# Expert rows scattered to their tokens' places tile by tile, and the final sums fed by eight plain loads and split over three engines

## The reference, cut to what matters

```python
g = flat @ shared_gate.T
u = flat @ shared_up.T
shared_out = jax.nn.sigmoid(g) * u @ shared_down.T
weights = jax.nn.softmax(flat @ router_w.T, axis=-1)
top_w, top_idx = jax.lax.top_k(weights, 2)
...
he = jax.nn.sigmoid(ge) * ue
de = jnp.einsum('nei,ehi->neh', he, wd)
routed = (comb[:, :, None] * de).sum(axis=1)
return x + shared_out + routed
```

## Time and profile before

| | |
|---|---|
| median of 3 runs | 720.56 us (720.54 to 720.6) |
| the profiled execution's own time | 722.7 us |
| its span, first to last instruction | 720.9 us |
| PE busy | 629.1 us, 87% |
| DVE busy | 516.7 us, 72% |
| ACT busy | 449.4 us, 62% |
| POOL (GpSimd) busy | 321.6 us, 45% |
| mean granted clock of TensorE | 0.941 of 2.4 GHz |
| indirect DMAs issued by POOL | 39 (L1424) and 32 (L1604) |
| first L1424 starts, last L1563 starts, last L1614 starts | 566.59, 663.89, 716.07 us |

### The profile page before, as it was taken

One profiled execution on the slowest core, in us unless ns is written; L12 is line 12 of the kernel. 1 busy time (PEld: TensorE's weight loads), 2 busy tenths in 40 slices (PEclk: granted clock), 3 DMA queues, 4 the chain that ended last, 5 costly groups with the idle time before them and its releaser, 6 DMA issues.

```text
span 720.9 us, 11913 instructions
## 1 busy us (share of the span) xinstructions
PE 629.1 (87%) x3851; PEld 259.9 (36%) x3864; DVE 516.7 (72%) x959; ACT 449.4 (62%) x609; POOL 321.6 (45%) x444
## 2 busy tenths in 40 slices
PE   4888999999999999999999996778899899998960
PEld 3622332332333323323323321133454456665420
DVE  2497888888888888888888898743638444444684
ACT  3553877877877878877877876664432367774000
POOL 5584326346346355355443403331734544430664
PEclk9856999999999999999999997689999999999995
DMA  8543254364364354363334320041895233342454
GB/s 289 175 124 95 71 153 139 83 169 132 86 168 130 93 163 129 93 162 108 108 94 129 108 89 30 31 109 49 201 223 125 51 113 117 118 114 78 147 174 146
DMA packets 65611, 88.61 MB, mean 123 GB/s; under 512 B 12576, under 2 KB 46112, under 8 KB 64528
## 3 DMA queue, kind: packets, MB, share of 16 engines
q1 hardware_dynamic: 60992, 69.64, 32.1%
q0 software_dynamic: 4560, 18.22, 11.0%
HBM read 63.75 MB, written 32.74 MB: 134 GB/s over the span
## 4 chain that ended last, share of the span: by engine, by line
PE 66%; DVE 13%; ACT 8%; issue 6%; DMA 4%; POOL 2%; another core or an unknown queue 0%; SPq 0%; POOLq 0%; ACTq 0%; DVEq 0%
PE PS L859 16%; PE PS L831 10%; PE PS L640 8%; PE PS L766 8%; PE PS L1489 6%; ACT E L845 5%; DVE MX L772 5%; PE PS L719 4%; PE PS L1067 4%; PE PS L1550 3%; PE PS L1317 3%; DVE ST L393 2%; DMA E<-scr_ys,SL 2%; PE PS L1447 1%; ACT BIG L508 1%
## 5 line engine op out<-in xcount | busy, mean ns | idle before, releaser
L772 DVE TENSOR_REDUCE MX<-PS 128x1 f32<-128x512 f32 x512 | 326.7, 683 | 53.9 <-PE PS L766 53.3
L845 ACT ACTIVATE E<-PS 128x1024 f32<-128x1024 f32 x256 | 259.5, 1021 | 80.3 <-PE PS L831 79.5
L859 PE MATMUL PS<-E,BIG 128*32 128x512 f32 x1024 | 140.4, 621 | 3.3 <-ACT E L845 3.2
L766 PE MATMUL PS<-BIG 53*128 53x512 f16 x512 | 123.1, 400 | 17.5 <-DVE MX L772 17.2
L831 PE MATMUL PS<-BIG 55*128 55x512 f16 x512 | 103.1, 398 | 24.2 <-ACT E L845 20.7
L674 POOL TENSOR_TENSOR ML<-BIG,ML 128x512 f32<-128x512 f32 x30 | 38.3, 1277 | 142.6 <-ACT BIG L650 142.6
L831 PEld LDWEIGHTS PS<-BIG 55*128 55x128 f16 x512 | 24.7, 93 | 169.6 <-ACT E L845 99.7
L650 ACT ACTIVATE BIG<-PS,BIG 128x256 f32<-128x256 f32 x64 | 36.1, 565 | 36.1 <-PE PS L640 29.5
L1424 POOL DMA_INDIRECT CT<-scr_yr,IX x39 | 37.0, 949 | 43.9 <-PE PS L1447 36.9
L1511 DVE SCALAR_TENSOR_TENSOR E<-WP,PS 128x352 bf16<-128x352 f32 x39 | 20.3, 521 | 50.4 <-ACT WP L1501 46.7
L1489 PE MATMUL PS<-BIG,CT 128*128 x312 | 54.2, 318 | 0.6 <-issue 0.4
(11 more groups left out here) (211 smaller groups left out, 850.8 us busy)
## 6 DMA issues: line engine op xcount, KB each, us to landing
scr_parts<-WP SPq DMA_DIRECT2D x96, 128.0 KB
BIG<-scr_parts SPq DMA_DIRECT2D x64, 192.0 KB
BIG<-in_we POOLq DMA_DIRECT2D x8, 1088.0 KB, 14.1
scr_u<-ML SPq DMA_DIRECT2D x32, 256.0 KB, 2.1
scr_ys<-XN SPq DMA_DIRECT2D x19, 256.0 KB
X<-in_x SPq DMA_DIRECT2D x8, 512.0 KB, 6.3
CT<-in_ctx SPq DMA_DIRECT2D x8, 512.0 KB, 5.9
ML<-scr_u SPq DMA_DIRECT2D x16, 256.0 KB
```

What stands on the lines that cost most here:

```text
L766: e.matmul(PS[:, yi[name] % 3, :], QK[rows, qb(u), 0, j0 + jj, 128 * tt:128 * tt + 128], QK[rows, qb(u), 1, j0 + jj, :], start=True, stop= ...
L772: e.tensor_reduce(MX[:, g % 2, c:c + 1], PS[:, yi[name] % 3, :], AX.X, ALU.max)\
L845: e.activation(E[:, st, 2 * jj:2 * jj + 2, :], PS[:, slot(name):slot(name) + 2, :], ACT.Exp, scale=1 / 1024).then_inc(s["rc"], 1)
L859: ins = e.matmul(PS[32 * hh:32 * hh + 32, AVB, :], VT[:, b % 2, st, 4 * (g % 4) + hh, :], E[:, st, hh, :], start=(st == 0), stop=(st == 3))
```

## The change

- The list of slots carries a sign: `tok` and `ntok` are the token number plus one, positive for choice 0 and negative for choice 1, and zero for a padding slot. `IX` (which token to gather) is made from it in three DVE steps, and four more (`places`) make `OX`: the row of `scr_ys` where the result belongs. `scr_ys` now has rows 0 to 2047 for choice 0 of each token, 2048 to 4095 for choice 1, and a row of its own for every padding slot.
- SP's plain stores of pairs are gone. POOL stores each tile by an indirect DMA (`place`), due at tb+j+1.48 and tb+j+1.92. An eviction waits for both stores of the pair before last.
- The 32 gathers of the tail are gone. SP loads `scr_ys` in 8 plain loads of 512 KB, once all stores have landed; choice 1's rows of a block of four row tiles come before choice 0's.
- Each row tile's sum is shared by three engines: ACT multiplies choice 1 by its weight (`weigh`), POOL adds that to `X` (`second`), DVE multiplies choice 0 by its weight and adds it (`first`). For row tiles 0 to 7 DVE's addition of the shared result comes first of all; for tiles 8 to 15 (`LATE`) it comes last.

```diff
+LATE = 8
-    ys = nc.dram_tensor("scr_ys", (128 * NTILE, T), BF, kind="Internal").ap()
+    ys = nc.dram_tensor("scr_ys", (2 * 2048 + 128 * NTILE, T), BF, kind="Internal").ap()
...
-        GB = [E[:, i, :, :].rearrange("p a t -> p (a t)").bitcast(BF)[:, 512 * j:512 * j + 512]
-              for i in (0, 3) for j in range(8)]
+        GB = [[big[:, 2048 * (2 * m + c):2048 * (2 * m + c) + 2048].rearrange("p (a t) -> p a t", a=4) for m in range(4)]
+              for c in range(2)]
+        GW = [E[:, i, j, :] for i in (0, 3) for j in range(4)]
...
@@ one_hots @@
-                    ins = e.tensor_tensor(o, o, tok.rearrange("p (s o) -> p s o", o=1).broadcast_to([128, 16, NTILE]),
-                                          ALU.mult)
+                    number = (tok, ntok)[c].rearrange("p (s o) -> p s o", o=1).broadcast_to([128, 16, NTILE])
+                    ins = e.tensor_tensor(o, o, number, ALU.mult)
@@ invert_slots @@
             def evac(e):
                 e.wait_ge(s["dn"], r + 1)
-                e.tensor_copy(IX[:, :], PS[:, bank, 0:NTILE]).then_inc(s["de"], 1)
+                dch.step(e, e.tensor_copy(IN, PS[:, bank, 0:NTILE]))
+                dch.step(e, e.scalar_tensor_tensor(IA, IN, -1.0, IN, ALU.mult, ALU.max))
+                e.tensor_scalar(IX[:, :], IA, 1.0, -1.0, ALU.max, ALU.add).then_inc(s["de"], 1)
             dve.at(when(item) + .1 * dt_, evac)
+
+            def places(e):
+                dch.step(e, e.scalar_tensor_tensor(IS, IN, 0.0, IS, ALU.is_equal, ALU.mult))
+                dch.step(e, e.tensor_scalar(IN, IN, 0.0, 2048.0, ALU.is_lt, ALU.mult))
+                dch.step(e, e.scalar_tensor_tensor(IA, IA, -1.0, IN, ALU.add, ALU.add))
+                e.tensor_tensor(OX[:, :], IA, IS, ALU.add).then_inc(s["ox"], 1)
+            dve.at(when(item) + .12 * dt_, places)
...
@@ constants @@
+            e.iota(ti[:, 16:16 + NTILE], [[128, NTILE]], base=4097, channel_multiplier=1).then_inc(s["i128"], 1)
...
+            e.tensor_copy(IS, ti[:, 16:16 + NTILE]).then_inc(s["i128"], 1)
...
+            e.tensor_scalar(ntok, tok, -1.0, None, ALU.mult).then_inc(s["i128"], 1)
...
@@ shared_down @@
-                e.wait_ge(s["ba"], 4 * blk + nt + 1)
-                acc = X[:, 4 * blk + nt, :]
+                i = 4 * blk + nt
+                if i >= LATE:
+                    e.wait_ge(s["ga"], i + 1)
+                else:
+                    e.wait_ge(s["ba"], i + 1)
+                acc = X[:, i, :]
                 e.scalar_tensor_tensor(acc, PS[:, bank, :], ZO, acc, ALU.mult, ALU.add).then_inc(s["de"], 1)
-            dve.at(tb + NP + 3.0 + 2 + 1.95 * last.index(item), evac)
+            i = last.index(item)
+            dve.at(tb + NP + 3.0 + max(2 * (i + 1), 9.7 + 1.3 * i if i >= LATE else 0), evac)
@@ down @@
                 if j >= 2 and a == 0:
-                    e.wait_ge(s_ys[j % 2], 16 * (j // 2))
+                    e.wait_ge(s_ys[j % 2], 32 * (j // 2))
                 e.tensor_scalar(YS[j % 2][:, a, :], PS[:, 4 + a, :], 0.5, None, ALU.mult).then_inc(s["de2"], 1)
             dve.at(tb + j + 1 + (.38 if a == 0 else .82), evac)
-            if a == 1 or r == NTILE - 1:
-                def store(e):
-                    e.wait_ge(s["de2"], r + 1)
-                    e.dma_start(ys[256 * j:128 * r + 128].rearrange("(a p) t -> p a t", p=128), YS[j % 2][:, 0:a + 1, :])\
-                        .then_inc(s_ys[j % 2], 16)
-                sp.at(tb + j + 1.9, store)
+
+            def place(e):
+                if r == 0:
+                    e.wait_ge(s["ox"], 1)
+                e.wait_ge(s["de2"], r + 1)
+                e.indirect_dma_start(ys, bass.IndirectOffsetOnAxis(ap=OX[:, r:r + 1], axis=0), YS[j % 2][:, a, :], None)\
+                    .then_inc(s_ys[j % 2], 16)
+            pool.at(tb + j + 1 + (.48 if a == 0 else .92), place)
@@ the tail @@
-        def gather(i, c):
...
-                e.indirect_dma_start(GB[n % 16], None, ys,
-                                     bass.IndirectOffsetOnAxis(ap=SL[:, c, i:i + 1], axis=0)).then_inc(s_g[n % 16], 16)
-            pool.at(te + n, f)
...
+        def fetch_rows(m, c):
+            def f(e):
+                if m == 0 and c:
+                    e.wait_ge(s_ys[0], 16 * 20)
+                    e.wait_ge(s_ys[1], 16 * 19)
+                rows = ys[2048 * c + 512 * m:2048 * c + 512 * m + 512]
+                e.dma_start(GB[c][m], rows.rearrange("(a p) t -> p a t", p=128)).then_inc(s_g[2 * m + c], 16)
+            sp.at(te + m + (0 if c else .5), f)
+
+        def combine(i):
+            m, a = i // 4, i % 4
+            late_sum = i >= LATE
+
+            def weigh(e):
+                e.wait_ge(s_g[2 * m + 1], 16)
+                if i == 0:
+                    e.wait_ge(s["top"], 2)
+                    e.wait_ge(s["h"], len(hq))
+                if i >= 8:
+                    e.wait_ge(s["gp"], i - 7)
+                e.activation(GW[i % 8], GB[1][m][:, a, :], ACT.Identity, scale=M8[:, i, 1:2]).then_inc(s["gw"], 1)
+            act.at(te + 1 + i, weigh)
+
+            def second(e):
+                e.wait_ge(s["gw"], i + 1)
+                if late_sum:
+                    e.wait_ge(s["ba"], i + 1)
+                else:
+                    e.wait_ge(s["de"], listed + i + 1)
+                e.tensor_tensor(X[:, i, :], X[:, i, :], GW[i % 8], ALU.add).then_inc(s["gp"], 1)
+            pool.at(te + 1 + i, second)
+
+            def first(e):
+                e.wait_ge(s_g[2 * m], 16)
+                e.wait_ge(s["gp"], i + 1)
+                ins = e.scalar_tensor_tensor(X[:, i, :], GB[0][m][:, a, :], M8[:, i, 0:1], X[:, i, :], ALU.mult, ALU.add)
+                ins.then_inc(s["ga"], 1)
+            dve.at(te + 9.6 + 1.3 * i, first)
+
+            def store(e):
+                if late_sum:
+                    e.wait_ge(s["de"], listed + i + 1)
+                else:
+                    e.wait_ge(s["ga"], i + 1)
+                e.dma_start(out[i // 2, 128 * (i % 2):128 * (i % 2) + 128, :], X[:, i, :]).then_inc(s["out"], 16)
+            sp.at(te + 20 + i, store)
```

More of the change, by code:

```diff
@@ L187, in xattn_moe @@
         i128 = bvB[:, 0:64].bitcast(HF)
-        tok = bvB[:, 64:72].bitcast(HF)
+        tok, ntok = (bvB[:, i:i + 8].bitcast(HF) for i in (64, 72))
         TI = bvB[:, 80:112].bitcast(U32)
@@ L201, in xattn_moe @@
         HE = E[:, 2, 0, 0:384].bitcast(BF).rearrange("p (a n) -> p a n", a=2)
-        GB = [E[:, i, :, :].rearrange("p a t -> p (a t)").bitcast(BF)[:, 512 * j:512 * j + 512]
-              for i in (0, 3) for j in range(8)]
+        GB = [[big[:, 2048 * (2 * m + c):2048 * (2 * m + c) + 2048].rearrange("p (a t) -> p a t", a=4) for m in range(4)]
+              for c in range(2)]
+        GW = [E[:, i, j, :] for i in (0, 3) for j in range(4)]
+        IA, IN, IS = (bvB[:, i:i + NTILE] for i in (80, 120, 200))
+        OX = bvB[:, 160:160 + NTILE].bitcast(U32)
         def qb(u):
@@ L225, in xattn_moe @@
         s_xs = [sem(f"xs{i}") for i in range(2)]
-        s_g = [sem(f"gth{i}") for i in range(16)]
+        s_g = [sem(f"gth{i}") for i in range(8)]
         pe, act, dve, pool, sp = (Queue() for _ in range(5))
@@ L1243, in one_hots @@
                 sf = SF.rearrange("p a b -> p (a b)")
-                e.wait_ge(s["i128"], 6)
+                e.wait_ge(s["i128"], 7)
                 e.wait_ge(s["gu"], tuse[3] + 1)
@@ L1286, in constants @@
             e.wait_ge(s["i128"], 2)
-            e.iota(ti[:, 0:16], [[128, 16]], base=0, channel_multiplier=1).then_inc(s["i128"], 1)
-            e.wait_ge(s["i128"], 3)
-            e.tensor_copy(tok, ti[:, 0:16]).then_inc(s["i128"], 3)
+            e.iota(ti[:, 0:16], [[128, 16]], base=1, channel_multiplier=1).then_inc(s["i128"], 1)
+            e.iota(ti[:, 16:16 + NTILE], [[128, NTILE]], base=4097, channel_multiplier=1).then_inc(s["i128"], 1)
+            e.wait_ge(s["i128"], 4)
+            e.tensor_copy(IS, ti[:, 16:16 + NTILE]).then_inc(s["i128"], 1)
+            e.tensor_copy(tok, ti[:, 0:16]).then_inc(s["i128"], 1)
             e.wait_ge(s["i128"], 6)
+            e.tensor_scalar(ntok, tok, -1.0, None, ALU.mult).then_inc(s["i128"], 1)
+            e.wait_ge(s["i128"], 7)
             e.memset(tri, 1.0).then_inc(s["tr"], 1)
@@ L1587, in xattn_moe @@
         te = tb + NP + 3.0
-        def landed(n):
-            return te + 3.2 + 1.25 * n
-        def gather(i, c):
-            n = 2 * i + c
+        def fetch_rows(m, c):
             def f(e):
-                if n == 0:
-                    e.wait_ge(s_ys[0], 8 * NP)
-                    e.wait_ge(s_ys[1], 8 * NP)
-                    e.wait_ge(s["h"], len(hq))
[L1600 to L1603, removed]
-                e.indirect_dma_start(GB[n % 16], None, ys,
-                                     bass.IndirectOffsetOnAxis(ap=SL[:, c, i:i + 1], axis=0)).then_inc(s_g[n % 16], 16)
-            pool.at(te + n, f)
-            def add(e):
-                e.wait_ge(s_g[n % 16], 16 * (n // 16 + 1))
```

(18 more changed lines are left out.)

## The result

The changed kernel takes 750.3 us (median of four runs, 748.8 to 752.4) against 720.6 before, a ratio of 1.041 (95% interval 1.038 to 1.044). The forecast was 731.0 with a range to 742: the sign is right, the size is not. The profiled execution has a span of 750.6 us against 720.9.

What follows compares the result with a forecast made beforehand. The prediction took the loop as bound by PE and the tail by 32 indirect gathers. Loop end 664.58 + 24 + tail 42.7 = 731.3 against 720.9, +10.4, so 731.0 from the 720.56 median; range 721 to 742.

Steps and rivals of the forecast that it cites:

- The list: Token list's eviction, before POOL's first gather: three dependent DVE steps instead of one, all on the path, 0.6 us.
- Store at the price of a gather: POOL in the loop: an indirect store issues like an indirect gather, 1.25 us from start to start.
- From eviction to the transposes of pair j+3: Loop: after tile (j, 0)'s eviction, store and gathers issue on POOL and rows land before pair j+3's transposes; 5.5 us.
- From transposes to the eviction of the next pair but one in the queue (j+2, 0): Loop: the round's other step, 6.0 us from a steady pair's timeline, making 11.5 us per two pairs instead of 8.92.
- The clock falls: Rival in the loop: PE, waiting about every second pair, is granted less clock; 10 us, total 741; chance 0.15.
- R: End of the loop's last DVE eviction: 664.58 before the change, forecast 688.6 after it.
- The tail, R+42.7, with its clash: After the loop: DVE operations with two SBUF inputs hold up POOL's adds, 1.7 to 1.92 us per tile; end R+42.7.
- no clash: Rival in the tail: POOL and DVE don't hold each other up, end R+36.7, total 725; chance 0.15.
- R+45.9: Tail's end by the skill's blocking rule alone, 1.27 + 0.75 us per tile; 3 us later than the forecast took.
- the lead holds: Rival in the loop: PE doesn't wait for gathers, only POOL's 5.0 us per pair binds; end 711.1 or 717.1; chance 0.12.

Runs made afterwards that it cites:

- experiment 4: Kernel before plus one wait: gathers of pair j+3 wait for the eviction of tile (j, 0), with no indirect stores; 757.3 us, ratio 1.045.
- changed, with filler: Changed kernel with 24 identity transposes ahead of each odd pair's transposes from pair 3 on, where PE waits for rows; 735.0 us, ratio 1.021, on chip C.
- experiment 3: Changed kernel with DVE's share of the final sum cut from 512 columns to 8 per row tile, all waits kept; 744.6 us.
- gathers first: Changed kernel with the gathers of pair j+3 ahead of the second store of pair j-1 in POOL's queue; 746.4 us, ratio 1.033, on chip A.
- the kernel with extra gathers: Kernel before with two more gathers a pair (pairs 3 to 19) into idle SBUF, read by nothing; 733.5 us, ratio 1.016.
- experiment 2: Changed kernel with SP's plain stores in slot order in place of the 39 indirect stores, so the tail sums wrong rows; 708.1 us, ratio 0.979.

## Why the prediction was wrong, by its own steps

- *The list, +0.6.* Three steps, first gather 0.5 us later relative to the eviction. Right.
- *Store at the price of a gather, 1.25 us start to start.* 1.29. Right.
- *From eviction to the transposes of pair j+3, 5.5 us.* 5.6 here, 5.7 in the mean of the eight rounds. Right, and so is the mechanism; experiment 4 shows the wait with no store in the kernel, at 1.5 us more than its own forecast.
- *"From transposes to the eviction of the next pair but one in the queue (j+2, 0) ... 6.0 us."* This is the step that failed. Measured 8.1 us in the mean of eight rounds, 16.6 us too much in all. The row behind the 6.0 is of a loop where PE never waits, and I carried it over to one where it waits 1.9 to 3.4 us for rows in each round. It holds only where the clock stays full and the release comes in time:

| kernel | rounds | granted clock in the step | the step, us |
|---|---|---|---|
| changed, the profile above | 4 | 1.00, tanh late | 7.6 to 8.1 |
| | 4 | 0.69 to 0.81, tanh late in 3 | 8.1 to 8.7 |
| changed, chip C | 7 | 0.78 to 0.81 | 7.3 to 7.7 |
| | 1 | 1.00 | 6.0 |
| changed, with filler, chip C | 8 | 1.00 | 6.0 |

- *"The clock falls", the rival that I gave 0.15 and priced at 10 us, 741.* On chips C and D, without late releases, the changed kernel takes 742.4 and 744.6 us, and on C the step is 11.5 us too long in all, at a fallen clock. That rival came true there, within 4 us; to hold it unlikely since "the waits here are shorter" was the misjudgement. It ought to have been in the sum.
- *What the loop's 17.6 us above the forecast are made of.* 16.6 are the step that failed; 1.6 the one from eviction to transposes; 1.0 the last stretch before R; and the start of the loop gave back 1.7. Late releases, which the forecast doesn't have at all, make the profile above 5 to 7 us longer than the loops of chips C and D (131.8 and 133.8). They don't simply add to the clock's price: in four of the eight rounds above the clock stayed full and the late tanh was the whole loss. Why it stayed full in those isn't shown.
- *The tail, R+42.7, with its clash.* R+41.5; adds of 1.62 us each, a little less than the 1.7 to 1.92 forecast. Right, "no clash" refuted by experiment 3. The end that I had worked out from the Trainium skill ("SBUF — State Buffer", § Who interferes with whom), R+45.9, is 4.4 us too late: the two operations do hold each other up, but a tile takes 1.62 us from add to add and not the 2.02 of one after the other.
- *The rival "the lead holds", 711 to 717.* Not this kernel, but one number away from it: gathers first, 716.9 and 715.6 on chips C and D; on A and E, with late releases, 746.4 and 743.2.
- *The range* ended at 742, as the slow cases were taken one at a time and at their first price. A stall that lowers the clock doesn't exclude any other loss. Even without late releases the kernel takes 742 to 745, just outside.

By the Trainium skill ("TensorE: Matmul & The Clock Gate", § HAM oscillation) a loop of short compute and DMA waits is throttled at each turn. The traces of the changed kernel on chips C and D agree, in seven and all eight of eight rounds; the profile above agrees in four of eight, and the others have their gate-up matmuls at 1.36 us, as at 686.29.

## What to carry to other kernels

Ask of each instruction put on a queue which independent ones stand behind it: a store that waits for a late result took away the lead of the gathers queued after it. A duration read between two events of a steady loop holds as long as nobody in it stalls; once PE waits, its own clock is part of the price, and idle matmuls in the wait can buy it back, less what they hold up themselves (here 11 us bought, 5 given away). Before a large gain or loss is put down to a kernel, run it on a second chip.

## What the hardware showed beyond that

- On two of the five chips of the experiments, and in the profiles of both kernels compared here, PE's releases can come late while POOL issues indirect DMAs back to back: some 2 to 5 us after the matmuls' end in rows of four to seven issues, 9.5 us in a row of eleven. Most come 0.6 to 1.6 us after the row's end, a few inside a row. The kernel before has one such place, behind the four gathers of 573.89 to 578.60: a copy of ACT at 579.65 had waited 3.0 us ("remote"). The kernel before takes 720 to 725 us on all five chips; gathers first, with twice the issues in its loop, takes 717 us on one and 746 on another.
- The cause stays open. Whether it lies in the chip or in its state at the time isn't known, and the kernel with extra gathers, which would tell how far gathers alone go, met no chip that shows it. On chip A itself the kernels with two issues in a row are free of it past the first gathers: plain stores (experiment 2, loop 98.0 us) and held gathers (experiment 4).
- Filler transposes in PE's waits raised the granted clock, from 590 to 690 us, from 0.88 to 0.98 in one kernel and from 0.89 to 0.98 in another.
